# Layer 0 of a two-layer convolution network: another order and other buffers for the second product, and both low parts of h on GpSimd

## The reference, cut to what matters

```python
# layer 0
h = conv 7x7 of each channel by itself, + conv_b
h = (h - mean over channels) * rsqrt(variance + 1e-5) * ln_g + ln_b
h = gelu(h @ w1 + b1, approximate=False)      # 96 -> 384 features
h = h @ w2 + b2                               # 384 -> 96
x = h * layer_scale + x
# layer 1: 5x5 conv of each channel, silu, a selective scan over the 3136 pixels, output
```

## Time and profile before

| what | value |
|---|---|
| median of three timed runs | 4056.53 us |
| profiled execution | 4053.06 us, span 4051.3 us |
| instructions in the span | 72657 |
| DMA | 613.07 MB, 151 GB/s in the mean |
| layer 0 / layer 1 | about 1845 us / about 2206 us |

### The profile page before, as it was taken

One profiled execution on the slowest core, in us unless ns is written; L12 is line 12 of the kernel. 1 busy time (PEld: TensorE's weight loads), 2 busy tenths in 40 slices (PEclk: granted clock), 3 DMA queues, 4 the chain that ended last, 5 costly groups with the idle time before them and its releaser, 6 DMA issues. The chain is left out here.

```text
span 4051.3 us, 72657 instructions
## 1 busy us (share of the span) xinstructions
PE 3669.9 (91%) x22358; PEld 2643.2 (65%) x22358; DVE 3170.4 (78%) x4640; ACT 2564.9 (63%) x4292; POOL 2309.4 (57%) x2448
## 2 busy tenths in 40 slices
PE   6999999999999999997899898998989989899776
PEld 6778787979787787867566564664646646556322
DVE  3676858585766768580399899998998989989999
ACT  1453718172645537274688788787877878778764
POOL 0232404141322324140398897988988889888988
PEclk9999999999999999997799898898988989989887
DMA  7546473746465464427565555564546646455321
GB/s 229 166 139 197 103 245 96 248 101 218 120 188 160 133 206 105 169 75 161 137 172 152 146 167 131 168 170 127 169 125 172 181 115 181 133 159 161 94 74 61
DMA packets 383776, 613.07 MB, mean 151 GB/s; under 512 B 199967, under 2 KB 324152, under 8 KB 383048
## 3 DMA queue, kind: packets, MB, share of 16 engines
q1 hardware_dynamic: 383336, 607.74, 52.7%
HBM read 527.35 MB, written 80.28 MB: 150 GB/s over the span
## 5 line engine op out<-in xcount | busy, mean ns | idle before, releaser
L523 ACT ACTIVATE act_h<-ps_up,b 128x448 f32<-128x448 f32 x672 | 408.9, 635 | 781.7 <-PE ps_up L641 781.4
L1354 PE MATMUL ps_y<-h,ident 128*128 128x448 f32 x1344 | 728.8, 630 | 148.3 <-POOL h L1042 118.5
L320 POOL TENSOR_TENSOR h_low<-act_h,h_high 128x448 fp32r<-128x448 f32 x224 | 287.6, 1284 | 901.4 <-ACT h_high L528 901.3
L1042 POOL TENSOR_TENSOR h<-h,c_rows 128x448 f32<-128x448 f32 x672 | 763.8, 1137 | 51.2 <-DVE h L1132 5.6
L1029 POOL TENSOR_TENSOR u<-dxs,b_rows 128x448 f32<-128x448 f32 x672 | 764.4, 1138 | 22.8 <-DVE ps_q L1121 14.7
L1105 DVE TENSOR_TENSOR_SCAN ps_q<-d_a,q_last,ps_q 128x448 f32<-128x448 f32 x576 | 659.7, 1145 | 0.0
L1132 DVE TENSOR_TENSOR_SCAN h<-d_a,h_last,ps_q 128x448 f32<-128x448 f32 x576 | 645.5, 1121 | 0.0
L1306 PEld LDWEIGHTS ps_front<-win,taps 120*112 120x112 f32 x4608 | 538.2, 187 | 148.3 <-issue 146.3
L614 PE MATMUL ps_stage<-win,taps 124*112 124x112 f32 x6144 | 608.0, 260 | 2.7 <-DVE w_low L367 2.7
L614 PEld LDWEIGHTS ps_stage<-win,taps 124*112 124x112 f32 x6144 | 607.8, 178 | 3.3 <-DVE w_low L367 2.8
L1211 ACT ACTIVATE d_a<-delta,log_eps,a_neg 128x448 f32<-128x448 f32 x672 | 503.4, 750 | 119.4 <-DVE h L1132 59.3
(11 more groups left out here) (82 smaller groups left out, 6267.3 us busy)
## 6 DMA issues: line engine op xcount, KB each, us to landing
taps<-in_t_dram SPq DMA_DIRECT2D x192, 896.0 KB, 5.1
taps<-in_t_dram SPq DMA_DIRECT2D x192, 672.0 KB, 4.6
b_rows<-bc_dram SPq DMA_DIRECT2D x224, 224.0 KB, 2.9
c_rows<-bc_dram SPq DMA_DIRECT2D x224, 224.0 KB, 3.1
xres<-in_x_dram SPq DMA_DIRECT2D x224, 168.0 KB, 2.5
x_dram<-x1o SPq DMA_DIRECT2D x224, 168.0 KB, 2.0
x1pad<-x_dram SPq DMA_DIRECT2D x96, 392.0 KB, 5.7
out_dram<-y SPq DMA_DIRECT2D x168, 224.0 KB, 2.7
```

Of the source, the lines that this page charges most:

```text
L523: nc.scalar.activation(act_h[u % 2][:, t, :], ps_up[t][:, 0:BT], ACT.Gelu, bias=b1[:, t:t + 1]).then_inc(gelu_done, 1)
L1042: nc.gpsimd.tensor_tensor(h[s % H_SLOTS][:, :], h[s % H_SLOTS][:, :], c_rows[n][:, :], ALU.mult).then_inc(hc_done, 1)
L1354: nc.tensor.matmul(total, ident[:, :], h[s % H_SLOTS][:, :], start=False, stop=(n == N - 1)).then_inc(y_added, 1)
```

## The change

The bank that `ps_back` loses goes to `ps_down`, so that there is one of the first and two of the second. `back(u)` now waits for `hn_low` of unit u - 1. `down(u)` waits for the residual of unit u - 2 in place of u - 1, and its products stand in another order: the four of `h_high` first, then the float32 one, then the two of `h_low`. Each product of `h_high` waits for ScalarE's `h_high`, where before it stood behind the wait for `h_low`. VectorE's `h_low` of tile 0 goes to GpSimd, which makes tile 0 and tile 1 one behind the other, each as soon as its `h_high` is there. No product and no element of work is added or left out.

```diff
-        ps_back = [pb(f"ps_back{i}") for i in range(2)]
+        ps_back = pb("ps_back")
-        ps_down = pb("ps_down")
+        ps_down = [pb(f"ps_down{i}") for i in range(2)]
...
             def h_low_part(g, u):                      # GpSimd
-                pool.wait_ge(h_high_ready, (g * UNITS + u) * FS + 2)
-                nc.gpsimd.tensor_tensor(h_low[u % 2][:, 1, :], act_h[u % 2][:, 1, :], h_high[u % 2][:, 1, :],
-                                        ALU.subtract).then_inc(h_low_ready[1], 1)
+                for t in range(FS):
+                    pool.wait_ge(h_high_ready, (g * UNITS + u) * FS + t + 1)
+                    nc.gpsimd.tensor_tensor(h_low[u % 2][:, t, :], act_h[u % 2][:, t, :], h_high[u % 2][:, t, :],
+                                            ALU.subtract).then_inc(h_low_ready[t], 1)
...
-            def h_low_part(g, u):                      # VectorE, with its three calls
-                dve.wait_ge(h_high_ready, (g * UNITS + u) * FS + 1)
-                nc.vector.tensor_tensor(h_low[u % 2][:, 0, :], act_h[u % 2][:, 0, :], h_high[u % 2][:, 0, :],
-                                        ALU.subtract).then_inc(h_low_ready[0], 1)
...
             def back(g, u):
                 pe.wait_ge(ln_scaled, g * CHUNKS + (u * BLKS + BLKS - 1) // CHUNK + 1)
-                if u >= 2:
-                    pe.wait_ge(hn_ready, g * UNITS + u - 1)
+                if u >= 1:
+                    pe.wait_ge(hn_ready, g * UNITS + u)
...
             def down(g, u):
-                pe.wait_ge(gelu_done, (g * UNITS + u + 1) * FT)
-                if u > 0:
-                    pe.wait_ge(x1_done, g * UNITS + u)
-                for t in range(FS, FT):
-                    nc.tensor.matmul(ps_down[0:C, 0:BT], w2[:, t, :], act_h[u % 2][:, t, :],
-                                     start=(t == FS), stop=False)
-                for t in range(FS):
-                    pe.wait_ge(h_low_ready[t], g * UNITS + u + 1)
-                    high, low = h_high[u % 2][:, t, :], h_low[u % 2][:, t, :]
-                    nc.tensor.matmul(ps_down[0:C, 0:BT], w2_part[0][:, t, :], high, start=False, stop=False)
-                    nc.tensor.matmul(ps_down[0:C, 0:BT], w2_part[1][:, t, :], high, start=False, stop=False)
-                    mm = nc.tensor.matmul(ps_down[0:C, 0:BT], w2_part[0][:, t, :], low,
-                                          start=False, stop=(t == FS - 1))
+                total = ps_down[u % 2][0:C, 0:BT]
+                if u >= 2:
+                    pe.wait_ge(x1_done, g * UNITS + u - 1)
+                for t in range(FS):
+                    pe.wait_ge(h_high_ready, (g * UNITS + u) * FS + t + 1)
+                    for part in range(2):
+                        nc.tensor.matmul(total, w2_part[part][:, t, :], h_high[u % 2][:, t, :],
+                                         start=(t == 0 and part == 0), stop=False)
+                for t in range(FS, FT):
+                    pe.wait_ge(gelu_done, (g * UNITS + u) * FT + t + 1)
+                    nc.tensor.matmul(total, w2[:, t, :], act_h[u % 2][:, t, :], start=False, stop=False)
+                for t in range(FS):
+                    pe.wait_ge(h_low_ready[t], g * UNITS + u + 1)
+                    mm = nc.tensor.matmul(total, w2_part[0][:, t, :], h_low[u % 2][:, t, :],
+                                          start=False, stop=(t == FS - 1))
                 mm.then_inc(down_done, 1)
```

More of the change, by code:

```diff
@@ L352, in split_weights @@
                 dve.wait_ge(shift_done, 1)
-                nc.vector.tensor_tensor(b1[:, :], b1[:, :], ps_down[:, 0:FT], ALU.add).then_inc(prepared, 1)
+                nc.vector.tensor_tensor(b1[:, :], b1[:, :], ps_down[0][:, 0:FT], ALU.add).then_inc(prepared, 1)
                 nc.vector.tensor_scalar(w1[:, :], w1[:, :], gain[:, 0:1], None, ALU.mult).then_inc(w1_scaled, 1)
@@ L411, in normed @@
                 dve.wait_ge(hn_high_ready, g * UNITS + u + 1)
-                nc.vector.tensor_tensor(hn_low[u % 2][:, :], ps_back[u % 2][0:C, 0:BT], hn_high[u % 2][:, :],
+                nc.vector.tensor_tensor(hn_low[u % 2][:, :], ps_back[0:C, 0:BT], hn_high[u % 2][:, :],
                                         ALU.subtract).then_inc(hn_ready, 1)
@@ L418, in residual @@
                 dve.wait_ge(x1_stored[u % 2], (g * (UNITS // 2) + u // 2 + 1) * 16)
-                nc.vector.scalar_tensor_tensor(x1o[u % 2][:, :], ps_down[0:C, 0:BT], b2[:, 0:1],
+                nc.vector.scalar_tensor_tensor(x1o[u % 2][:, :], ps_down[u % 2][0:C, 0:BT], b2[:, 0:1],
                                                xres[u % 2][:, :], ALU.add, ALU.add).then_inc(x1_done, 1)
-            def h_low_part(g, u):
-                dve.wait_ge(h_high_ready, (g * UNITS + u) * FS + 1)
-                nc.vector.tensor_tensor(h_low[u % 2][:, 0, :], act_h[u % 2][:, 0, :], h_high[u % 2][:, 0, :],
-                                        ALU.subtract).then_inc(h_low_ready[0], 1)
             def keep_conv(g):
@@ L442, in begin @@
                 a, b = HELD_UNITS
-                for c, step in ((0, 0), (0, 1), (1, 0), (0, 2), (1, 1), ("h_low", a), (0, 3), (0, 4), ("windows", 0),
-                                (1, 2), ("h_low", b), ("residual", a), (0, 5), ("windows", 2), ("normed", 0),
+                for c, step in ((0, 0), (0, 1), (1, 0), (0, 2), (1, 1), (0, 3), (0, 4), ("windows", 0),
+                                (1, 2), ("residual", a), (0, 5), ("windows", 2), ("normed", 0),
                                 ("windows", 4), (1, 3), (1, 4), (2, 0), (2, 1), ("residual", b), (1, 5),
@@ L448, in begin @@
                         normed(g, 0)
-                    elif c == "h_low":
-                        if held:
-                            h_low_part(g - 1, step)
                     elif c == "residual":
@@ L472, in unit @@
                         ln(g, c, step)
-                h_low_part(g, u)
             def group(g, after):
@@ L514, in hn_high_part @@
                 act.wait_ge(back_done, g * UNITS + u + 1)
-                nc.scalar.activation(hn_high[u % 2][:, :], ps_back[u % 2][0:C, 0:BT],
+                nc.scalar.activation(hn_high[u % 2][:, :], ps_back[0:C, 0:BT],
                                      ACT.Copy).then_inc(hn_high_ready, 1)
@@ L623, in back @@
                 pe.wait_ge(ln_scaled, g * CHUNKS + (u * BLKS + BLKS - 1) // CHUNK + 1)
-                if u >= 2:
-                    pe.wait_ge(hn_ready, g * UNITS + u - 1)
+                if u >= 1:
+                    pe.wait_ge(hn_ready, g * UNITS + u)
                 for j in range(BLKS):
-                    mm = nc.tensor.transpose(ps_back[u % 2][0:C, j * TOK:(j + 1) * TOK],
+                    mm = nc.tensor.transpose(ps_back[0:C, j * TOK:(j + 1) * TOK],
                                              conv[:, u * BLKS + j, :], ident[0:TOK, 0:TOK])
@@ L706, in _ @@
             for t in range(FT):
-                mm = nc.tensor.matmul(ps_down[:, t:t + 1], w1[:, t * 128:(t + 1) * 128], shift[:, 0:1],
+                mm = nc.tensor.matmul(ps_down[0][:, t:t + 1], w1[:, t * 128:(t + 1) * 128], shift[:, 0:1],
                                       start=True, stop=True)
```

## The result

The changed kernel took 4026.49 us in the median of 16 runs (4005.15 to 4044.03), the kernel before 4056.94 in the median of 16 (4037.60 to 4072.58). The ratio is 0.9925, with a 95% interval of 0.9908 to 0.9941: 30 us faster, where 43 were forecast. The profiled execution has a span of 4018.6 us, 32.7 less than before.

The account below looks back on a forecast made before the run. TensorE was taken as busiest, its stalls in layer 0's units ending at waits for `h_low` and the residual. 35 us from seven groups and 8 from the last, 43 off 4053.06, gave 4010 us; range 3992 to 4066, the forecast's own 3995 to 4028.

Parts of the forecast that it names:

- the two waits of `down`: In the units, `down` waits for the residual and for `h_low`; all named stalls end there, at most 64 us.
- the last group: Eighth group, without windows: 2.2 of 3.61 us of stalls go in each of 3.5 periods, 8 us less.
- One `ps_back`, more waits on TensorE: 0: `back(u + 1)` waits for `hn_low` of unit u, as `up(u)` already did: 0; added waits in `down`: 0, at most 22 us.
- Moving the subtraction relieves VectorE: In the units, `h_low` of tile 0 on GpSimd takes 0.54 us a unit off VectorE, and GpSimd keeps up.
- The walk through units 5 to 8: Units followed with the durations of before: 0.3 us of stall stays at unit 8, 0.7 of 2.23 a period.
- About 3.3 periods: Between unit 3 and a group's end, 3.3 periods each win 1.5 us: 35 us over seven groups.
- The start: 0, either way 0 to 1: At a group's start, `down` of the last unit waits for GpSimd instead of the residual: 0 to 1 us, taken as 0.
- GpSimd keeps the way for its pair: Rival, chance 0.20: in the units line 406 waits for both GpSimd subtractions, +16 us, 4069 us.
- Half the gain: Rival, chance 0.16: in the units stalls move to `hn_low` and meetings eat the rest, or added waits show; 4032 us.
- more than 28.3 us to unit 2: From the convolution's end; sign of the rival that each group's start gets 2 us longer, 4046 us, chance 0.10.

Follow-up runs that it names:

- the short subtractions: The changed kernel with GpSimd's two subtractions cut to 8 of 448 columns, the rest of `h_low` left zero; 3959.34 us in one run.

## Why the prediction was right, and where it was not

The sign was right, and half of the mechanism: the two waits of `down` went from the units, the relief of VectorE did not come as forecast. The size was 30 us for 43 (42.4 before rounding). In the profiled executions, 32.7 us: the units of seven groups 7 x (1.11 + 0.14 + 0.29 + 0.87) = 16.9 where 35 were forecast, the last group 3.1 where 8 were, the starts 6.8 and layer 1 7.9 where the forecast had 0, and 2.0 lost ahead of unit 3 of the first group. So the terms that the forecast summed brought 20 us of 43, and 13 more came from where it had 0: that 4026 lies in its own range (3995 to 4028) is in part luck. Of the 16 us between 4010 and 4026, 4 are the base, since the kernel before has a median of 4056.94 and the sum began at 4053.06.

*The two waits of `down`.* Right in the units: there both are gone. Behind the convolutions `down` still waits for `h_low`, now GpSimd's (17.6 us in all). Banks and order without anything else give 17.5 us. The order does most of it, the bank alone nothing.

*One `ps_back`, more waits on TensorE: 0.* Right: `back` waits for line 407 and never for `hn_low`, and dense units still take 4.17 and 4.83 us, now with all waits in place.

*Moving the subtraction relieves VectorE.* Wrong. The walk took 0.54 us a unit off VectorE's list, 121 us in 224 units, and left 0.7 of stalls a period for the meetings. VectorE's busy time in layer 0 fell by 62.5 us only (1225.78 to 1163.33). Line 406, at 1222 ns in the median and 1816 at the most, is at 1444 and 2903; line 391 (now 392), which makes the means, has a median of 846 in place of 172; GpSimd's subtraction is as before in the median, and its power went from 1820 to 1480:

```profile
L407 DVE TENSOR_TENSOR conv<-conv,ln_rstd x128: 843/1444/2903, 143.7 to 1794.5; 112x672 f32<-112x672 f32 x128
...
L392 DVE TENSOR_SCALAR ln_mean<-ln_sum x128: 164/846/1129, 139.1 to 1787.2; 112x7 f32<-112x7 f32 x128
...
L321 POOL TENSOR_TENSOR h_low<-act_h,h_high x448: 1126/1153/1902, 153.7 to 1807.7; 128x448 fp32r<-128x448 f32 x150
...
L315 POOL TENSOR_TENSOR ln_rstd<-ln_var,minus_half x128: 1477/1480/2020, 142.2 to 1792.8; 112x7 f32<-112x7 f32 x128
```

Half of the relief came back as waiting, and in places where TensorE feels it: alone, the move costs layer 0 14.6 us. The last group shows it best: 31.94 a period where 30.7 were forecast, and 31.25 with banks and order alone.

*The walk through units 5 to 8.* The place was right: what remains ends at `hn_low` of unit 8, which the prediction had, with 0.44 us for its 0.3. Unit 6 was to lose its 0.26 and kept it: 5.09 in the mean, where it is 4.75 with banks and order alone and with the short subtractions. Ahead of it, in each of the seven groups, stands a multiplication of 2.55 to 2.57 us that waited for both of GpSimd's subtractions. Unit 7 takes 4.96 (4.47 forecast), unit 9 is dense. In all 1.1 goes where 1.5 was forecast.

*"About 3.3 periods" of the same gain.* This is the step of the sum that failed, the term of 35 us: the other two periods of a group gave 0.14 and 0.29 in place of 1.5 each. The prediction read units 3 to 9 of one group, and no row of SyncE's queue. Loading two images in quarters brings back 0.52 and 1.14 us, 7 x 1.66 = 11.6 us of the 18 missing in the units.

*The start: 0, either way 0 to 1.* The profile has 0.97 less a group in the mean. Starts vary by more within a kernel, but the four whole kernels with new banks and order and both subtractions always on GpSimd have means of 30.76 to 31.41, the four that leave tile 0 to VectorE in ordinary units 31.84 to 32.30. So the second subtraction does seem to shorten the start. As the kernel with both on GpSimd only there did not show it (31.91), why is open.

*The rivals.* "GpSimd keeps the way for its pair" was to decide from a mean of line 406 above 2 us; it is 1.43. As a sum it is wrong, as a mechanism it is there, and two of its signs came: instances near 3 us, and `back` waiting for the multiplication (16.4 us in 25 places; 17.8 in 45 with banks and order alone, so this second sign does not need the pair). Two pairs 6 us apart in the kernel after show both outcomes, first GpSimd's row and then VectorE's of each:

```profile
396.71 2.26 POOL L321 TENSOR_TENSOR h_low<-act_h,h_high 128x448 fp32r<-128x448 f32 x2
...
402.77 2.86 POOL L321 TENSOR_TENSOR h_low<-act_h,h_high 128x448 fp32r<-128x448 f32 x2
```

```profile
397.13 2.56 DVE L407 TENSOR_TENSOR conv<-conv,ln_rstd 112x672 f32<-112x672 f32 x1
...
402.83 1.80 DVE L407 TENSOR_TENSOR conv<-conv,ln_rstd 112x672 f32<-112x672 f32 x1 [0.28 <-POOL ln_rstd L315]
```

In the first, GpSimd did both without a break (2.26 us) and VectorE waited for both; in the second VectorE got in between, and GpSimd's pair is longer by 0.6. Of the 128 instances 52 are below 0.95 us and were not held up. The other 76 met such a pair: in 66 VectorE got in between (53 of them take 1.7 to 1.9 us), in 10 it waited for both. These 10 are not spread at random. Seven are those ahead of unit 6; three, of 2.90 us, stand at the beginning of units 6, 13 and 20 of the last group, which take 5.51 us each where they take 4.82 with banks and order alone. That is as much as the whole difference in the last group, 3 x 0.69 of 2.08 us. What decides who goes is not seen: at 859.47 VectorE is 0.06 us behind GpSimd and gets in between, at 1707.70 it is 0.06 behind and waits for both.

"Half the gain", 4032 us, is nearer to the measured 4026.5 than the forecast's 4010 is, and its mechanism, stalls that move to `hn_low` while each meeting eats the rest, is a good part of what happened.

What this profile was to show: no wait of `down` (right in the units), units 3 to 9 in about 32.7 us (33.03), `hn_low` at 3.2 us after a unit's start except in unit 7 (3.1 in units 3 to 5, 3.55 in unit 6, 4.22 in unit 7, 4.3 and 5.0 in units 10 and 11), the mean of line 406 at 1.3 and no instance above 1.9 (1.43, and 10 longer ones), GpSimd near 80% in the units (74%), and more than 28.3 us to unit 2 as a sign against (816.28 - 789.78 = 26.5, with the first product behind the convolution at 789.78).

## What to carry to other kernels

Put the operand that is made last into the last products of an accumulation before looking for a faster engine for it; here that order gave more than the bank, and moving the subtraction alone lost. Work moved from VectorE to GpSimd may come back as waiting where the two meet, here half of it: price it by the instructions that it will meet, not by its own length, and try it with the moved work made short. When a rival's average does not come true, look for its single instances and where they stand. A gain found in one period may be multiplied only after the others have been read too, with the queue of the engine that issues the transfers; a wait that cost nothing before can become the bound after the change.

## What the runs showed of the hardware

- A meeting holds up a whole instruction. With GpSimd's subtractions short, all 128 multiplications take 836 to 860 ns; with two of 1.15 us a unit the median is 1444 ns. The Trainium skill, "GPSIMD Engine Reference", section "8. Key points", has the two contend for their SBUF interfaces; the trace agrees and adds that against two GpSimd instructions in a row VectorE got in between in 66 of 76 places and waited for both in 10.
- A store issued right behind a whole image's load takes 5.9 to 7.7 us to issue in 14 places of the kernel after, behind two quarters 1.0 to 2.3 us, elsewhere 0.34. The loads behind it in the same queue are late by as much.
- Layer 1, which no kernel here changes, took 2215 to 2231 us at a mean granted clock of 0.88 or 0.89 and, where layer 0 loads images in quarters, 2240 to 2263 us at 0.86 to 0.88. A gain in one part of a program has to be measured over the whole.
